# Routed experts: weighted rows added straight into the result instead of stored, read back and combined

## The reference

```python
def _L1_ffn_ref(x, router_w, w1, b1, w2, b2):          # x = LN(h), 2208 x 256
    router_probs = softmax(x_flat @ router_w.T)         # 8 experts
    top_k_probs, top_k_idx = top_k(router_probs, 2)
    top_k_probs = top_k_probs / (top_k_probs.sum(axis=-1, keepdims=True) + 1e-08)
    cw = (one_hot(top_k_idx, E) * top_k_probs[..., None]).sum(axis=1)
    output = zeros_like(x_flat)
    for e in range(E):
        h = new_gelu(x_flat @ w1[e].T + b1[e])          # 1024 wide
        out_e = h @ w2[e].T + b2[e]
        output = output + cw[:, e:e + 1] * out_e
    return output
...
h = h + _L1_ffn_ref(LN(h), ...)                         # the result
```

## Time and profile before

| | us |
|---|---|
| median of 3 runs (1175.94 to 1181.26) | 1179.62 |
| the profiled execution, its own time | 1180.71 |
| its span, first to last instruction | 1178.9 |
| PE busy | 973.6 (83% of the span) |
| DVE busy | 643.8 (55%) |
| POOL busy | 647.4 (55%) |
| ACT busy | 576.6 (49%) |

### The profile page before, as it was taken

How to read it: one execution, slowest core, us unless ns; L and a number is a source line. 1 busy time by engine, 2 the same in 40 slices (tenths; PEclk the granted TensorE clock), 3 DMA queues, 4 the chain that set the end, 5 groups by cost and what they waited for, 6 DMA issues and landing times. The chain is left out here.

```text
span 1178.9 us, 21890 instructions
## 1 busy us (share of the span) xinstructions
PE 973.6 (83%) x6860; PEld 868.1 (74%) x6860; DVE 643.8 (55%) x1439; ACT 576.6 (49%) x1175; POOL 647.4 (55%) x623
## 2 busy tenths in 40 slices
PE   6269699997899999688887799993199999999970
PEld 5258377776788988466666699992199999999970
DVE  1335599994465563499996355543633333333335
ACT  0021277775355565333443456652166676666640
POOL 0115488875355553244333699861167777777750
PEclk9679899997799999878888799995589999999995
DMA  7661344441111111000000600007246666666656
GB/s 249 181 248 50 86 139 158 157 159 44 54 55 55 55 55 55 1 0 1 0 0 9 283 2 14 28 15 279 99 140 197 194 205 182 204 193 202 198 169 230
DMA packets 64749, 136.93 MB, mean 116 GB/s; under 512 B 12361, under 2 KB 26434, under 8 KB 63346
## 3 DMA queue, kind: packets, MB, share of 16 engines
q1 hardware_dynamic: 55698, 113.32, 29.8%
q0 software_dynamic: 4848, 14.72, 3.6%
q10 hardware_dynamic: 4144, 8.16, 1.9%
HBM read 114.01 MB, written 24.39 MB: 117 GB/s over the span
## 5 line engine op out<-in xcount | busy, mean ns | idle before, releaser
L121 DVE CAST place<-place 128x512 fp32r<-128x512 f32 (+3 forms) x188 | 107.4, 609 | 176.0 <-PE moe_down L127 100.5
L2273 POOL TENSOR_TENSOR place<-place,place 128x512 fp32r<-128x512 f32 x84 | 138.3, 1646 | 52.2 <-DVE place L121 52.2
L2299 PE MATMUL moe_up<-place,place 128*128 128x128 f32 x1376 | 163.3, 278 | 0.0
L2299 PEld LDWEIGHTS moe_up<-place,place 128*128 128x128 f32 x1376 | 159.8, 195 | 0.0
L127 PE MATMUL moe_down<-place,place 128*128 128x256 f32 x1008 | 130.8, 286 | 0.0
L127 PEld LDWEIGHTS moe_down<-place,place 128*128 128x128 f32 x1008 | 123.3, 191 | 0.0
L2358 ACT ACTIVATE place<-place 128x2048 f32 x44 | 84.0, 1912 | 44.0 <-PEq L2095 29.9
L2371 ACT ACTIVATE place<-moe_up,place 128x128 f32<-128x128 f32 x344 | 97.5, 366 | 15.2 <-POOL place L2273 14.7
L1423 POOL TENSOR_TENSOR place<-place,place 128x384 fp32r<-128x384 f32 x42 | 43.7, 1043 | 89.3 <-ACT place L1330 62.4
L1528 POOL TENSOR_TENSOR place<-place,place 69x1024 f32<-69x1024 f32 x16 | 30.9, 1929 | 93.1 <-DVE place L167 93.1
L785 PE MATMUL scores<-place,place 128*69 128x276 f32 x256 | 68.5, 412 | 11.1 <-DVE place L849 6.8
(11 more groups left out here) (271 smaller groups left out, 2128.5 us busy)
## 6 DMA issues: line engine op xcount, KB each, us to landing
place<-w_remainder SPq DMA_DIRECT2D x172, 256.0 KB, 4.0
place<-in_w_dram SPq DMA_DIRECT2D x4, 4096.0 KB, 12.9
place<-gate_rows SPq DMA_DIRECT2D x24, 384.0 KB, 4.8
place<-in_w_dram SPq DMA_DIRECT2D x16, 512.0 KB, 3.8
w_remainder<-place SPq DMA_DIRECT2D x16, 512.0 KB, 3.0
place<-value_rows SPq DMA_DIRECT2D x64, 64.0 KB, 2.8
place<-choices ACTq DMA_DIRECT2D x5, 768.0 KB, 7.1
place<-in_patches_dram SPq DMA_DIRECT2D x9, 384.0 KB, 3.8
```

The source lines that it names most:

```text
L121: return eng.tensor_copy(out, x)
L2273: pool.tensor_tensor(lo[f], raw[f], hi[f].bitcast(F32), ALU.subtract).then_inc(h_split, 1)
L2299: last = pe.matmul(p1[u][k // HK][:, (k % HK) * P:(k % HK + 1) * P], ws[u][:, c, k * P:(k + 1) * P], xT[u][:, c, :], start=(c == 0), stop= ...
```

## The change

`combine` and the table `choices` go. The result in HBM first gets `h` and then each routed row is added to it in place, already multiplied with its weight.

1. `second_feed`: after each group's rows of x, SP also stores the group's rows of `h` to the result (six DMAs of 384 KB).
2. `xn_rows` gets rows of 258 numbers. `route_second` writes the token's two weights into the last two columns (one DMA of 2304 pieces of 8 bytes), and the block ends when that has landed.
3. `routed`: the gather brings 258 numbers. DVE picks the slot's own weight out of the two (`weigh`, two dependent instructions of one column per block), POOL's next load waits for it. DVE multiplies the bias row with the weight (one more instruction), and the last step out of PSUM becomes a multiply-add. The store becomes an indirect DMA that adds to the result. Empty slots go to 128 spare rows ahead of it. `aim` computes the targets before the loop, nine instructions of 44 columns.
4. SP's loop runs 41 times instead of 42, without the reload that nobody read.

```diff
@@ second_feed, SP
-                    sp.dma_start(rows[:, G * g:G * g + G, :], of(x, g)).then_inc(xn_out, 16)
+                    sp.dma_start(rows[:, G * g:G * g + G, 0:D], of(x, g)).then_inc(xn_out, 16)
+                    sp.dma_start(out_rows[:, G * g:G * g + G, :], of(h, g)).then_inc(h_out, 16)
@@ route_second, SP
+                sp.wait_ge(weighed, 1)
+                sp.dma_start(self.xn_rows[:, D:D + 2].rearrange("(a p) k -> p a k", p=P), self.weight).then_inc(weights_out, 16)
+                sp.wait_ge(weights_out, 16)
                 sp.wait_ge(self.xn_out, 16 * NG)
+                sp.wait_ge(self.h_out, 16 * NG)
@@ routed, POOL
                     if n >= 1:
                         pool.wait_ge(stored[(n - 1) % 2], 16 * ((n - 1) // 2 + 1))
-                    pool.indirect_dma_start(out=self.choices, out_offset=bass.IndirectOffsetOnAxis(ap=self.target[:, n:n + 1], axis=0),
-                                            in_=y[n % 2], in_offset=None).then_inc(stored[n % 2], 16)
+                    pool.indirect_dma_start(out=self.out, out_offset=bass.IndirectOffsetOnAxis(ap=self.target[:, n:n + 1], axis=0),
+                                            in_=y[n % 2], in_offset=None, compute_op=ALU.add).then_inc(stored[n % 2], 16)
...
                         if f == 0 and n + 4 < XBLK:
                             pool.wait_ge(tx_mm, n + 3)
+                            pool.wait_ge(weighed, n + 3)
                             load(n + 4)
@@ routed, DVE
+                def weigh(n, i, u):
+                    dve.wait_ge(xg_in[u], i * 16 + 16)
+                    at = bass.ds(n, 1)
+                    dve.tensor_tensor(part[:, at], xg[u][:, D:D + 1], self.choice[0][:, at], ALU.mult).then_inc(parted, 1)
+                    dve.wait_ge(parted, n + 1)
+                    dve.scalar_tensor_tensor(out=own[:, at], in0=xg[u][:, D + 1:D + 2], scalar=self.choice[1][:, at], in1=part[:, at],
+                                             op0=ALU.mult, op1=ALU.add).then_inc(weighed, 1)
...
+                dve.wait_ge(spare_in, 16)
+                aim()
+                weigh(0, 0, 0)
+                weigh(1, 0, 1)
                 split(0, 0, owner_of(dve, 0))
                 with dve.Fori(0, NBLK // 2) as i:
                     for u in range(2):
                         n = i * 2 + u
                         e, following = owner_of(dve, n), owner_of(dve, n + 1)
+                        weigh(n + 2, i + 1, u)
                         dve.wait_ge(quarter_mm[3], n)
                         split(n, 1, e)
                         dve.wait_ge(quarter_mm[1], n + 1)
                         split(n + 1, 0, following)
+                        dve.tensor_scalar(w2_bw, w2_b[:, bass.ds(e, 1), :].rearrange("p a d -> p (a d)"), own[:, bass.ds(n, 1)], None,
+                                          ALU.mult).then_inc(biased, 1)
+                        dve.wait_ge(biased, n + 1)
                         dve.wait_ge(quarter_mm[3], n + 1)
                         dve.wait_ge(stored[u], i * 16)
-                        dve.tensor_tensor(y[u], p2[:, 0:D], w2_b[:, bass.ds(e, 1), :].rearrange("p a d -> p (a d)"), ALU.add).then_inc(y_read, 1)
+                        dve.scalar_tensor_tensor(out=y[u], in0=p2[:, 0:D], scalar=own[:, bass.ds(n, 1)], in1=w2_bw,
+                                                 op0=ALU.mult, op1=ALU.add).then_inc(y_read, 1)
@@ routed, SP
-                with sp.Fori(0, NBLK) as n:
+                with sp.Fori(0, NBLK - 1) as n:
@@ run
-        self.combine()
```

More of the change, by code:

```diff
@@ L1746, in _ @@
                 rows = self.xn_rows.rearrange("(a p) d -> p a d", p=P)
+                out_rows = self.out[P:P + NT * P, :].rearrange("(a p) d -> p a d", p=P)
                 half = E * KF // 2
@@ L2075, in route_second @@
         self.source, self.target = m.take(XBLK).bitcast(U32), m.take(XBLK).bitcast(U32)
-        self.weight = [m.take(NT) for _ in range(2)]
+        self.parity = m.take(XBLK).bitcast(U32)
+        spent = self.lg.rearrange("p a e -> p (a e)")
+        self.slot_row, self.choice = spent[:, 0:XBLK], [spent[:, k * XBLK:(k + 1) * XBLK] for k in (1, 2)]
         self.owner = m.take(XBLK).bitcast(U32)
@@ L2090, in route_second @@
         rows = [m.take(NT * XBLK).bitcast(mybir.dt.bfloat16).rearrange("p (a g b) -> p a g b", g=2, b=XBLK) for _ in range(2)]
-        row = m.take(XBLK)
+        row, past_row = self.slot_row, m.take(XBLK)
+        self.weight = m.take(NT, 2)
         exped, step = sem("route2_exp"), sem("route2_step")
         hit, ranked, hot_ready, table_mm = sem("hits_ready"), sem("ranks_mm"), sem("slot_rows_ready"), sem("slot_table_mm")
+        weighed, weights_out = sem("route2_weights"), sem("route2_weights_out")
         lg = self.lg
@@ L2120, in _ @@
                 link(dve.tensor_tensor(lg, lg, inner(total, E), ALU.mult))
-                self.choose(lg, first, second, self.weight, tmp, dve, link)
+                self.choose(lg, first, second, [self.weight[:, :, k] for k in range(2)], tmp, dve, link)
                 link(dve.tensor_tensor(tmp, first, second, ALU.add))
                 dve.tensor_tensor(hits, tmp, inner(consts["valid"], E), ALU.mult).then_inc(hit, 1)
-                link(dve.tensor_tensor(total, self.weight[0], self.weight[1], ALU.add))
+                link(dve.tensor_tensor(total, self.weight[:, :, 0], self.weight[:, :, 1], ALU.add))
                 link(dve.tensor_scalar(total, total, 1e-8, None, ALU.add))
                 link(dve.reciprocal(total, total))
-                for w in self.weight:
-                    link(dve.tensor_tensor(w, w, total, ALU.mult))
+                dve.tensor_tensor(self.weight, self.weight, inner(total, 2), ALU.mult).then_inc(weighed, 1)
                 dve.wait_ge(ranked, 1)
@@ L2198, in routed @@
         assert m.pos <= self.xn_at + NT * D
+        m.at(0)
+        xg = [m.take(D + 2) for _ in range(2)]
+        own, part, w2_bw = m.take(XBLK), m.take(XBLK), m.take(D)
+        where, empty, spare_row = m.take(XBLK), m.take(XBLK), m.take(1)
+        assert m.pos <= NT * D
         m.at(self.route_at)
@@ L2201, in routed @@
         w1_b = m.take(E * KF)
-        xg = [m.take(D) for _ in range(2)]
         xT = [m.take(C, P) for _ in range(2)]
@@ L2335, in split, with aim @@
                     leading(dve, w2_hi[f], w2).then_inc(w2_cut, 1)
+                def weigh(n, i, u):
[5 more added lines that the diff above has]
+                                             op0=ALU.mult, op1=ALU.add).then_inc(weighed, 1)
+                def aim():
+                    link = Steps(dve, aimed, 0)
+                    link(dve.tensor_copy(self.choice[1], self.parity))
+                    link(dve.tensor_scalar(self.choice[0], self.choice[1], -1.0, 1.0, ALU.mult, ALU.add))
+                    link(dve.tensor_scalar(where, self.slot_row, 1.0, None, ALU.add))
+                    link(dve.tensor_copy(self.target, where))
+                    link(dve.tensor_scalar(self.target, self.target, 1, None, ALU.logical_shift_right))
+                    link(dve.tensor_copy(where, self.target))
+                    link(dve.tensor_scalar(empty, self.slot_row, 0.0, spare_row, ALU.is_equal, ALU.mult))
+                    link(dve.scalar_tensor_tensor(out=where, in0=where, scalar=float(P - 1), in1=empty, op0=ALU.add, op1=ALU.add))
+                    link(dve.tensor_copy(self.target, where))
+                dve.wait_ge(spare_in, 16)
+                aim()
+                weigh(0, 0, 0)
+                weigh(1, 0, 1)
                 split(0, 0, owner_of(dve, 0))
@@ L2385, in _ @@
                             hidden(n + 1, 1 - u, e, f)
[L2388 to L2415, removed]
-                            dve.scalar_tensor_tensor(out=self.h[0:n, a, :], in0=got[0:n, a, c, :], scalar=self.weight[c][0:n, a:a + 1],
-                                                     in1=self.h[0:n, a, :], op0=ALU.mult, op1=ALU.add).then_inc(mixed, 1)
-                            if c == 0:
-                                dve.wait_ge(mixed, 2 * a + 1)
-            @block.sync
-            def _(sp):
-                for a, b in parts:
-                    n, t0, t1 = tiles(a, b)
-                    sp.wait_ge(mixed, 2 * b)
-                    sp.dma_start(self.out[t0:t1, :].rearrange("(a p) d -> p a d", p=n), self.h[0:n, a:b, :]).then_inc(stored, 16)
-                sp.wait_ge(stored, 16 * len(parts))
     def load_route_consts(self, sp):
@@ L2538 @@
         dram[key] = nc.dram_tensor(f"in_{key}_dram", a.shape, mybir.dt.from_np(a.dtype), kind="ExternalInput").ap()
[L2539 removed]
+    out = nc.dram_tensor("out_0_dram", [P + NT * P, D], F32, kind="ExternalOutput").ap()
     build(nc, dram, out)
```

24 lines of the change are left out of this document (14 added, 10 removed).

## The result

The changed kernel takes 1236.21 us (median of 4 runs, 1232.85 to 1240.98) against 1178.95 us of the kernel before on the same chip: 1.049 times the time, 95% interval 1.0444 to 1.0537. The forecast was 1161 us with a range to 1180. So the sign was wrong, and 75 us of the time were not foreseen.

A forecast was written before the change was run, and what follows sets the result against it. The prediction took the loop to be bound by PE, busy 278.00 of 278.00 us. 1180.7 - 23.0 + 2.8 + 1.8 - 0.2 = 1162.1, for the median 1161 us; range 1154 to 1180, own range 1155 to 1173.

The forecast's parts named there:

- `combine`, the tail and the routing block: Outside the loop: 23.0 us saved by dropping `combine`, 1.8 added by the last store's landing, 0.2 saved in routing.
- The closing stretch: 8.88 us without work after POOL's last store, kept in the forecast; rival: partly `combine`'s, up to 5 us shorter, chance 0.04.
- +2.8: Loop: PE's second product stalls 0.13 us for POOL's remainder in each of 21 pairs of blocks, 2.8 us in all.
- `weigh` itself, taken as 0.65: DVE's two dependent instructions ahead of POOL's gather: between 0.42 and 0.9 us, taken as 0.65.
- The remainder without a cast beside it, 1.30: POOL's remainder of half 1 after the gather: 1.30 us without DVE's cast beside it, 1.65 with it.
- 1104.23 + 0.65 + 0.98 = 1105.86: Block u = 0: `weigh` starts at 1104.23, takes 0.65 us, then the gather's issue takes 0.98, ending at 1105.86.
- the chain through `weigh` is longer: Loop rival: `weigh` at 0.9 and remainder at 1.65 us make the stall 13.4 instead of 2.8 us, 1172 us; chance 0.08.
- The bias product ... some 0.3 us, and DVE waits 0.43 and 0.53 us for PE right there: DVE's 256-column bias product before the evict: some 0.3 us, covered by DVE's waits for PE, so no added time.
- the rival at 0.14: Loop: the adding store outlasts a block of 6.66 us, so POOL waits for the store before; 1216 us at 8 us; chance 0.14.
- the rival on DVE's casts: Loop: DVE's casts hold up POOL's gather issue, making the remainder late; 28 us, 1187 us; chance 0.05.
- The weights column: Routing block: 2304 pieces land in 14.4 us, 4.8 us early, or 28.8 and 9.6 late; late-landing rival, chance 0.06.
- a sign of a wrong forecast: Loop: PE's second product waiting for POOL's remainder by more than 0.5 us a pair would show the longer chain.

The follow-up runs named there:

- e5: Changed kernel with `weigh` one block ahead and the bias product earlier, both behind `split(n, 1)`, where DVE waits for PE; nothing left out: 1154.9 us.
- e1: Changed kernel with a plain, overwriting store in place of the adding one, leaving out the sum of a token's two rows: 1213.3 us.
- e6: Changed kernel with `weigh` and the bias product both moved, and a plain store in place of the adding one: 1151.5 us.
- e9: Changed kernel with `weigh(n + 2)` behind `split(n, 1)` of the same block instead of ahead of it, the gather still waiting for it: 1259.4 us.
- e4: Changed kernel with only the bias product moved, to behind `split(n, 1)`, where DVE waits for PE; `weigh` stays in place: 1191.7 us.
- e8: Changed kernel with the bias product in its old place over 8 of 256 columns, the bias of the others left out: 1231.4 us.
- e2: Changed kernel without the bias product, the bias row added unweighted: 1197.2 us.
- e3: Changed kernel with only `weigh` moved, one block ahead and behind `split(n, 1)`; the bias product stays in place: 1176.2 us.

## Why the prediction was wrong

**What goes: right, slightly low.** `combine`, the tail and the routing block were to be worth 23.0 - 1.8 + 0.2 = 21.4 us. With the loop bound by PE again (e5) the whole gain is 1179.8 - 1154.9 = 24.9. The tail is where it differs: from the last evict to the end e5 takes 25.6 us less (36.6 against 11.0), where 23.0 - 1.8 = 21.2 was forecast. The 1.8 us more for the last landing did not come, and from the start of the last store to the end of `routed` it was 10.95 us before (1144.93 to 1155.88) and is 8.3 now (1222.74 to 1231.0). The closing stretch, a rival at 0.04, did get shorter, but not only for the reason given there: with plain stores and no `combine` (e1, e6) it is still 10.0 us. Why it is shorter behind an adding store is open.

**The loop: wrong, +2.8 against +81** (1236.2 - 1154.9). The terms:

- *`weigh` itself, taken as 0.65:* right, 0.55. *The remainder without a cast beside it, 1.30:* right, 1.28.
- *"1104.23 + 0.65 + 0.98 = 1105.86": the step that failed first.* It lets the gather start where `weigh` ends. POOL starts 0.75 us later, whatever DVE does (e9). Before, the gather's conditions had been met for long, so it followed its predecessor by 0.1 to 0.2 us and no such gap stood in the rows of the loop. Outside of it the trace had the 0.27 us of the gather at 854.61; even that was left out of the sum, and it would have been too little. By my own margins, 0.13 us late for u = 0 and 0.13 early for u = 1, the gap makes 0.88 + 0.62 a pair, 21 x 1.50 = 31.5 us. Kernel e4, which has this chain and not the product in it, lies 36.8 above e5; the 5 us between the two stay unexplained. The rival "the chain through `weigh` is longer" named the place and had 13.4 us as its ceiling: it varied `weigh`'s size and not the hand-over.
- *"The bias product ... some 0.3 us, and DVE waits 0.43 and 0.53 us for PE right there": the larger failure.* Alone it is 0.35 us, so the size was right and the cover wrong. DVE's free time there is time in which POOL subtracts: the trace of before has it, ahead of the evict at 1102.29, in a row that I did not look at:

```profile
1101.34 1.65 POOL L2273 TENSOR_TENSOR place<-place,place 128x512 fp32r<-128x512 f32 x1 [0.77 <-DVE place L121]
```

It covers all of the 0.43 us that DVE waits there. The evict itself, which reads PSUM, lies inside this remainder and is not held: 0.42 us, as in all 42 blocks of before. The product has both ends in SBUF and stood until POOL was through, 2.40 us. Moving it to where POOL issues its gather gives 44.5 us (e4).

- *The adding store's price was put on its landing.* 5.5 us was taken, 4.9 us from issue to landing is the median of the 42, no store waited but the tail's, and the rival at 0.14 did not occur. The number was near by luck: it stood on a plain store at 5.46 us, and a plain store to the same rows lands in 2.5 (e1), so that adding costs 2.4 us, not nothing. And the issue on POOL is 1.59 us instead of 1.00, a term that was not in the sum. It is worth 23 us (e1), because it stands in the ring, ahead of the remainder that holds the product.
- *"0.95 late for u = 0, and 0.4 for u = 1"*, in the rival on DVE's casts: by its own rows the second is 1097.82 + 1.03 + 0.98 + 1.30 - 1100.58 = 0.55, and the rival's price 31.5 us instead of 28. Nothing hung on it.

**The rival about the lock was aimed the wrong way.** I weighed whether DVE's casts hold up POOL's gather (0.05), found no sign in the earlier trace rows, and put the rule of the Trainium skill aside. The same section ("SBUF — State Buffer", SBUF: two separate sides) also says that POOL holds up DVE, and there the change had put a new DVE operation. A quarter of a microsecond looked harmless; its size did not matter (e8).

**The weights column** was in time, as forecast. It was issued at 820.54 and the routing block ended at 842.88. It landed in 5.8 us, against the 14.4 that I reckoned (KB each, median us to landing):

```profile
xn_rows<-place SPq DMA_DIRECT2D x1, 18.0 KB, 5.8
```

By the Trainium skill's rule on transfers below 512 B ("DMA: Bandwidth & Descriptors", Specifications) I had put 28.8 us beside it; the measurement is far below, so reading the rule as twice my price for a piece was wrong here.

What was predicted as a sign of a wrong forecast did show: PE's second product waiting for POOL's remainder by more than 0.5 us a pair (2.11 in the block above). The sign named for right, stores without a wait for a DMA, showed as well, and told nothing.

## What to carry to other kernels

When you put an operation into an engine's idle time, look at what the other engine on the same SBUF ports does in that interval: here a VectorE operation with its operands in SBUF, beside GpSimd's subtraction, cost the rest of that instruction and not its own size. And when a wait is added ahead of an instruction that was always released early, price the hand-over to that engine (here 0.75 us into a GpSimd DMA), not only the work waited for. Both were cured by place, with no work removed: `weigh` a block ahead, the product earlier in its block, each in a stretch where VectorE waited for PE.

## What the runs showed that I had not expected

- An 8-column multiply takes 2.28 us beside POOL's subtraction and a 1-column one 1.25; the 256-column multiply alone takes 0.35.
- POOL starts a gather 0.75 to 0.78 us after the end of the `weigh` that it waited for, in all 40 of each of six kernels (the changed one, e1, e2, e4, e8, e9), but 0.27 us after PE's transposition before the change (854.61).
- An indirect store that adds takes 1.59 us to issue against 1.00 for the plain one, for the same 128 rows, and lands in 4.9 us against 2.5 (medians of 42, the changed kernel and e1).
- One piece, three prices: the longer issue was worth 23 us in the ring and 3.4 us beside PE (e6). The three single edits of the changed kernel (e3 60, e4 44.5, e1 23 us) add up to 127 us, where the loop had lost 81.
